# A decoder layer on one core: four split casts of the next batch's x moved by a few slots, and two down parts moved to the end of the last pair

## The reference, cut to what matters

```python
def attn(x):        # x: 4 x 512 x 512, 16 heads of 32, causal
    q, k, v = x @ Wq + bq, x @ Wk + bk, x @ Wv + bv
    q, k = rope(q), rope(k)
    return softmax(mask(q @ k.T / sqrt(32))) @ v @ Wo + bo
def cross(x, ctx):  # ctx: 4 x 512 x 256
    q, k = ctx @ Wq.T + bq, ctx @ Wk.T + bk
    return x @ softmax(q @ k.T)          # over the rows of one batch
def ffn(x):         # hidden 2048
    return (silu(x @ w_gate.T) * (x @ w_up.T)) @ w_down.T
x = layernorm(x + attn(x))
x = layernorm(x + cross(x, ctx))
x = layernorm(x + ffn(x))
```

## Time and profile before

| | |
|---|---|
| median of 3 runs | 979.93 us (978.96 to 980.32) |
| profiled execution | 980.25 us, span 978.5 us |
| mean granted TensorE clock | 0.989 |
| busy, share of the span | PE 96%, PEld 78%, DVE 74%, ACT 52%, POOL 61% |

### The profile page before, as it was taken

How to read it: one execution, slowest core, us unless ns; L and a number is a source line. 1 busy time by engine, 2 the same in 40 slices (tenths; PEclk the granted TensorE clock), 3 DMA queues, 4 the chain that set the end, 5 groups by cost and what they waited for, 6 DMA issues and landing times.

```text
span 978.5 us, 16194 instructions
## 1 busy us (share of the span) xinstructions
PE 935.2 (96%) x5272; PEld 760.8 (78%) x5272; DVE 726.6 (74%) x1588; ACT 513.1 (52%) x1150; POOL 598.0 (61%) x645
## 2 busy tenths in 40 slices
PE   7888999999999978998999999999999999999997
PEld 5666887888788766887878888888878888888885
DVE  5566778768877876679777777777877877767767
ACT  4576777777777776656244443343533263333333
POOL 2466745845774545457567775667846776665644
PEclk9997999999999999999999999999999999999999
DMA  6885665966666790012202111011112123111102
GB/s 217 246 206 151 193 164 157 260 164 166 193 193 176 199 286 2 23 44 108 65 0 65 43 54 65 33 65 65 32 33 66 33 108 108 35 63 65 33 33 87
DMA packets 40739, 105.20 MB, mean 108 GB/s; under 512 B 4944, under 2 KB 5072, under 8 KB 38608
## 3 DMA queue, kind: packets, MB, share of 16 engines
q1 hardware_dynamic: 40656, 104.16, 36.3%
HBM read 78.98 MB, written 25.17 MB: 106 GB/s over the span
## 4 chain that ended last, share of the span: by engine, by line
PE 73%; DVE 8%; ACT 7%; POOL 6%; issue 4%; DMA 2%; SPq 0%; POOLq 0%; DVEq 0%; ACTq 0%
PE pd L708 26%; PE pj L656 13%; PE pj L708 10%; PE pg L708 5%; PE pu L708 5%; PE pv L699 4%; PE ps L671 3%; PE pa L684 2%; PE pb L684 2%; ACT prob L898 2%; POOL raw L1457 1%; POOL raw L1462 1%; DMA qk_scratch<-raw 1%; ACT e L942 1%; POOL raw L1466 1%
## 5 line engine op out<-in xcount | busy, mean ns | idle before, releaser
L898 ACT ACTIVATE prob<-prob,nmax 128x512 f32<-128x512 f32 (+3 forms) x256 | 143.8, 562 | 75.8 <-DVE nmax L1162 74.9
L1162 DVE CUSTOM_DVE_ANT_0 prob<-ps,mask 128x512 f32<-128x512 f32 (+3 forms) x256 | 124.1, 487 | 78.0 <-PE ps L671 72.4
L671 PE MATMUL ps<-ks,qs 128*128 128x256 f32 (+2 forms) x256 | 105.9, 415 | 6.8 <-DVE nmax L1162 5.0
L1624 POOL TENSOR_TENSOR g_lo<-gated,g_hi 128x512 fp32r<-128x512 f32 x32 | 49.5, 1548 | 95.3 <-ACT g_hi L1002 95.3
L1457 POOL TENSOR_TENSOR raw<-raw,cos 128x512 f32<-128x512 f32 x32 | 42.4, 1324 | 99.2 <-DVE pj L1144 82.9
L1295 DVE TENSOR_TENSOR xb<-pd,xb 128x512 f32<-128x512 f32 x116 | 79.4, 685 | 27.2 <-PE pd L708 27.2
L1617 POOL TENSOR_TENSOR wop_lo<-wsum,wop_hi 128x512 fp32r<-128x512 f32 x64 | 81.7, 1301 | 1.3 <-ACT wop_hi L987 1.3
L1002 ACT CAST g_hi<-gated 128x512 fp32r<-128x512 f32 x32 | 19.9, 622 | 112.2 <-DVE gated L1355 112.2
L708 PE MATMUL pd<-dn_hi,g_hi 128*128 128x512 f32 x244 | 75.4, 390 | 2.4 <-POOL g_lo L1624 1.1
L708 PE MATMUL pd<-dn_lo,g_hi 128*128 128x512 f32 x244 | 75.1, 389 | 0.0
L708 PE MATMUL pd<-dn_hi,g_lo 128*128 128x512 f32 x244 | 75.1, 389 | 0.0
(11 more groups left out here) (525 smaller groups left out, 2818.0 us busy)
## 6 DMA issues: line engine op xcount, KB each, us to landing
f_raw<-in_w_ffn SPq DMA_DIRECT2D x32, 768.0 KB, 4.2
qs<-qk_scratch SPq DMA_DIRECT2D x64, 256.0 KB, 4.6
ks<-qk_scratch SPq DMA_DIRECT2D x60, 256.0 KB, 7.3
qk_scratch<-qk_hi SPq DMA_DIRECT2D x32, 256.0 KB, 2.0
qk_scratch<-raw SPq DMA_DIRECT2D x32, 256.0 KB, 2.2
res<-in_x SPq DMA_DIRECT2D x4, 1024.0 KB, 5.0
x_scratch<-res SPq DMA_DIRECT2D x4, 1024.0 KB, 5.4
xb<-x_scratch SPq DMA_DIRECT2D x4, 1024.0 KB, 5.8
```

Source lines behind the costliest of these rows:

```text
L671: pe.matmul(ps[:, t % 2, 0:w], qs[n % 2][:, r, s * P:(s + 1) * P], ks[n % 2][:, r, 0:w], start=True, stop=True).then_inc(s_done, 1)
L898: act.activation(prob[:, t % PROBS, 0:w], prob[:, t % PROBS, 0:w], ACT.Exp, bias=nmax[:, n % 2, i:i + 1], scale=-1.0, accum_out=rsum[:, n ...
L1162: dve.tensor_tensor_reduce(prob[:, t % PROBS, 0:w], ps[:, t % 2, 0:w], mask[:, S - w:S], -D ** -0.5, 3e38, ALU.add, ALU.min, accum_out=nma ...
L1624: pool.tensor_tensor(lo, (gated, gated_b)[b][:], hi.bitcast(F32), ALU.subtract).then_inc((glo_done, glo_b_done)[b], 1)
```

## The change

It does four things. In the attention stage tiles 0 to 3 of the next x are split at 29, 31, 34 and 36 where they were split at 27, 28, 34 and 35, and tiles 2 and 3 are loaded at 30 and 32 where they were loaded at 28 and 29. In the last step of the feed-forward stage the parts (c-1, 1, 0) and (c-1, 1, 1) leave their places among the products and stand directly in front of (c, 1, 0) and (c, 1, 1). The normalization of the last tile is made in two halves of 256 columns, and its store in two DMAs. No arithmetic is added or left out.

```diff
-LOAD_X = (10, 11, 28, 29)
-SPLIT_X = (27, 28, 34, 35)
+LOAD_X = (10, 11, 30, 32)
+SPLIT_X = (29, 31, 34, 36)
...
-        sp.wait_ge(ln_done[1], 1)
-        sp.dma_start(out[(B - 1) * P:B * P, (ST - 1) * E:ST * E], xb[B - 1][:, ST - 1, :]).then_inc(out_done, 16)
-        sp.wait_ge(out_done, 16 * (2 + 2 * ST))
+        for n in range(2):
+            sp.wait_ge(ln_done[1], n + 1)
+            cols = slice(2 * n * P, 2 * (n + 1) * P)
+            sp.dma_start(out[(B - 1) * P:B * P, (ST - 1) * E + 2 * n * P:(ST - 1) * E + 2 * (n + 1) * P],
+                         xb[B - 1][:, ST - 1, cols]).then_inc(out_done, 16)
+        sp.wait_ge(out_done, 16 * (3 + 2 * ST))
...
         product(h, "p2")
-        parts_ready(c - 1, 1)
-        pe.wait_ge(part_added, 2 * ST * (c - 1) + ST - 1)
-        part(c - 1, 1, 0, tail_bank(ST), True, False)
         product(h, "p5")
         product(h, "p4")
-        pe.wait_ge(part_added, 2 * ST * (c - 1) + ST)
-        part(c - 1, 1, 1, tail_bank(ST + 1), True, False)
         product(h, "p3")
+        parts_ready(c - 1, 1)
         pe.wait_ge(u2_done, NH)
         part(c - 1, 1, 2, tail_bank(ST + 2), True, False)
...
-        parts_ready(c, 1)
+        pe.wait_ge(part_added, 2 * ST * (c - 1) + ST)
         for s in range(ST):
+            if s < 2:
+                part(c - 1, 1, s, tail_bank(ST + s), True, False)
+            if s == 0:
+                parts_ready(c, 1)
             part(c, 1, s, tail_bank(ST + s), False, True).then_inc(tile_full, 1)
...
-        dve.tensor_scalar(xb[B - 1][:, s, :], xb[B - 1][:, s, :], mv2[1][:, at, 0:1], rstd2[1][:, at, :],
-                          ALU.subtract, ALU.mult).then_inc(ln_done[1], 1)
+        for cols in (slice(0, 2 * P), slice(2 * P, E)):
+            dve.tensor_scalar(xb[B - 1][:, s, cols], xb[B - 1][:, s, cols], mv2[1][:, at, 0:1], rstd2[1][:, at, :],
+                              ALU.subtract, ALU.mult).then_inc(ln_done[1], 1)
```

## The result

The changed kernel took 973.47 us (median of 5 runs, 971.95 to 975.33) against 980.08 us (5 runs) before: 6.6 us less, a ratio of 0.9932 with a 95% interval of 0.9915 to 0.9949. The forecast was 974.4.

What follows compares the result with a forecast made beforehand. TensorE, 96% busy, was taken to lose time waiting for ScalarE's copy out of pa, and VectorE to bound the last step. Terms 1.33 + 1.33 + 1.3 + 0.6 + 0.8 + 0.15 = 5.5 us gave 974.4, range 972.4 to 976.8.

Steps and rivals of the forecast that it cites:

- the first stretch: Attention stage, near 77 to 83 us: k's addition on GpSimd starts earlier, TensorE's waits shrink; 1.3 us, plus 0.6 for the clock.
- the last step: End of the feed-forward stage: moving two parts lets VectorE start the last tile 0.8 us earlier, with TensorE reaching g_lo just in time.
- the halves: Last tile's normalization and store in two pieces: 0.15 us won, bounds 0.1 lost and 0.5 won.
- Second and third stretch: Attention stage, periods into groups 5 and 9: TensorE's wait for the copy out of pa goes whole, 1.33 us each.
- The clock's term: First stretch: TensorE's low clock falls again but may come back near 83.3 us; 0.6 us won, ends 0 and 1.6.
- x itself as the next late thing: All three stretches: x's tile 3 comes later, leaving 0.3 us of slack; its load may take 4.2 us before TensorE waits.
- rival C: A new wait, from late low parts of x, row maxima or g_lo, takes part of the gain: 976.5 to 977.5 us, 8%.
- rival E: Slower: tile 3's load, directly ahead of eight stacked loads, is slowed by them, at 9.4 us landing giving 990; 5%.

Runs made afterwards that it cites:

- tiles 1 and 3 earlier: The changed kernel with x's tile 1 split at 30 instead of 31 and tile 3 loaded at 31 instead of 32: 975.0 us, ratio 0.9954 to the kernel before.

## Why the prediction was right

The direction, the places and the size held (974.4 forecast, 973.47 measured). Of the terms, the first stretch gave 1.3 us more than forecast, the last step and the halves 0.35 less together, and the late tile 3 of x was put at nothing. So the small miss of 0.9 us is what errors of either sign left over.

- **Second and third stretch**, forecast 1.33 each: 1.33 and 1.34. With GpSimd's low parts alone moved the periods are just as short, so the cause was the place of k's addition in GpSimd's queue.
- **First stretch**, forecast 1.3 plus 0.6 for the clock, the clock's ends 0 and 1.6: measured 3.2. Both terms were too small, because they are not separate. The 0.90 us of wait that I took was what was left of it while TensorE ran at half clock; with the short low clock it is 1.58. The waits themselves went as forecast: the second is down to 0.21 us, the first shrank by 0.2, from 1.13 to 0.92. So with the short low clock on both sides the stretch gives 1.65 to 1.85 us (22.29 less 20.44 to 20.64) and not 1.3. The clock's term comes on top: three of four profiles with the old slots have 10.2 us at low clock and cost 1.55 us more than the one with 3.4 (23.85 less 22.29), its upper end. My reason for it was half right: I expected the clock back near 83.3 us; it was back at 79.2 to 81.3, and what was left of it costs nothing (20.45 and 20.49 us without any low clock, 20.44 to 20.64 with 3.4 us of it). Why it lasts 10.2 us in one profile and 3.4 in another is open. With the old slots it began 13.7 to 13.8 us behind the start of group 0's product in the three long cases and 15.0 in the short one; with the new slots it began 13.9 to 15.0 behind and was short each time.
- **x itself as the next late thing**, forecast with 0.3 us of slack and a limit of 4.2 us for the landing: the wait is real, and it is what rival C has as low parts of x that come late, here through the load that rival E names. The new slots of both engines leave SP's order in the stretches the same in seven profiles. Of their 21 landings of tile 3, four took 4.3 to 5.2 us, and each lengthened its period (by 0.36, 0.7, 1.3 and 1.6 us). A landing less what it lengthened its period by is 3.6 to 3.9 us, so the limit lies there and not at 4.2. I had given this no term in the sum, only rivals; in the profile shown it took 0.74 back. That the eight loads directly behind make it late, as rival E has it, is not shown: the experiment meant to move them away left them in place, the same order gave anything from 2.7 to 5.2 us, and with them 1.7 us behind (tiles 1 and 3 earlier) all six landings were 3.9 to 4.2. With the old slots, where tile 2's load goes ahead and a store of k follows 1.9 us later, eleven of twelve landings took 2.7 to 3.4 us and one 4.1.
- **The last step**, forecast 0.8: 0.6 to 0.7. TensorE did come to g_lo just as it was ready, and part (c, 0, 0) took 1.50 us (951.07 to 952.57) instead of 1.36, where I allowed 0.05.
- **The halves**, forecast 0.15 won: 0.05 lost. I put 0.28 us for each half, and both take 0.73, 0.18 more than the one instruction. The second store is issued 0.08 us behind its normalization instead of 0.02, about as forecast, and lands in 2.02 us instead of 2.21.

With these sizes the sum is 3.2 + 1.33 + 1.34 + 0.65 - 0.05 = 6.5 us, less what a late tile 3 takes back in some runs, against 6.6 measured. The 3.2 holds for a kernel before with the long low clock. Which case the runs without a profile fell in is not known, so how closely the sum meets the medians is in part luck.

## What to carry to other kernels

An engine that works its list in order and carries work for two chains, one urgent and one not, is worth reading slot by slot: here two subtractions of 1.3 us each, ahead of an urgent addition in GpSimd's queue, lengthened each of three periods by 1.3 us and more, though GpSimd is busy only 61% of the time. What is pushed back then loses its slack, and a load whose buffer is freed later also lands later: price that load with its longest landing, not with its median. A wait read while TensorE runs at half clock is too short a price for it: at full clock the same wait was 1.58 us instead of 0.90. Where runs of one kernel spread over 3 us, judge parts of a change by distances between two instructions of one trace; the periods into groups 5 and 9 repeated here within 0.05 us, the long distance to the last tile within 0.2. And before an experiment with moved slots is read, compare the order in the engine's own list: a slot number can change and the order stay.

## What was not expected of the hardware

The same instruction stream had its low clock (half of full speed, 1.2 of 2.4 GHz) around 77 us for 10.2 us in three profiles and for 3.4 us in one. With 3.4 us of low clock in the changed kernel TensorE lost nothing, since VectorE and ScalarE hold that stretch: at full clock it waited 1.06 us where it had waited 0.21. A load of 256 KB, with eight more loads issued directly behind it in the same queue each time, took 2.7 to 3.6 us to land in 17 cases and 4.3 to 5.2 us in four; what decides between them is open. One VectorE instruction on 512 columns took 0.55 us, two on 256 took 0.73.
